# Four prologues of a gated delta rule kernel, from a counted loop to one written-out sequence

## The reference, cut to what matters

```python
    x = L0_attn_x
    xn = _layernorm(x, axis=-1)
    x = x + _L0_attn_ref(xn, ...) + _L0_ffn_ref(xn, L0_ffn_w_gate_up, L0_ffn_w_proj)
    return x
```

```python
        gu = jnp.einsum('bsd,hd->bsh', x, wq_gu)
        gate, up = jnp.split(gu, 2, axis=-1)
        h = jax.nn.silu(gate) * up
        hn = rms_norm(h)
        wq_p = ternary_quant(w_proj)
        return jnp.einsum('bsh,dh->bsd', hn, wq_p)
```

```python
            beta = jax.nn.sigmoid(b_raw.astype(jnp.float32))
            g = -A[None, None, :] * jax.nn.softplus(a.astype(jnp.float32) + dt_bias[None, None, :])
...
            g = jnp.cumsum(g.reshape(Bq, H, nc, chunk_size), axis=-1)
```

## Time and profile before

| | us |
|---|---|
| median of three runs | 5176.98 (5168.34 to 5177.32) |
| the profiled execution | 5178.37 |
| its span in the trace | 5176.3 |
| PE busy | 4793.5 (93%) |
| DVE busy | 3623.3 (70%) |
| ACT busy | 3024.5 (58%) |
| POOL busy | 1086.0 (21%) |

### The profile page before, as it was taken

One profiled execution on the slowest core, in us unless ns is written; L12 is line 12 of the kernel. 1 busy time (PEld: TensorE's weight loads), 2 busy tenths in 40 slices (PEclk: granted clock), 3 DMA queues, 4 the chain that ended last, 5 costly groups with the idle time before them and its releaser, 6 DMA issues.

```text
span 5176.3 us, 140889 instructions
## 1 busy us (share of the span) xinstructions
PE 4793.5 (93%) x52272; PEld 3332.8 (64%) x52272; DVE 3623.3 (70%) x6423; ACT 3024.5 (58%) x7909; POOL 1086.0 (21%) x1064
## 2 busy tenths in 40 slices
PE   2777799999999999999999999999999999999998
PEld 1545566666666666666666666666666666666666
DVE  6444477777777677777777767777777777777776
ACT  1222466666666656666666666666666666666665
POOL 0000122222222222222222222222222222222222
PEclk9888899999999999999999999999999999999999
DMA  1111222222222322222222222222222322222221
GB/s 50 31 30 30 82 57 64 53 54 64 57 65 52 79 63 58 64 52 55 64 57 73 68 55 63 58 65 52 57 63 68 77 52 58 61 63 58 64 52 35
DMA packets 686346, 300.56 MB, mean 58 GB/s; under 512 B 599152, under 2 KB 642288, under 8 KB 675440
## 3 DMA queue, kind: packets, MB, share of 16 engines
q1 hardware_dynamic: 546416, 283.18, 21.2%
q10 hardware_dynamic: 139264, 8.42, 1.8%
HBM read 212.76 MB, written 66.07 MB: 54 GB/s over the span
## 4 chain that ended last, share of the span: by engine, by line
issue 51%; PE 26%; POOL 12%; DVE 4%; DMA 3%; ACT 2%; SPq 1%; ACTq 1%; POOLq 0%; DVEq 0%
POOL sdec L1432 5%; PE pj L620 4%; POOL rout L1438 4%; PE dsb L757 3%; PE ms L678 2%; POOL kn L1425 2%; PE pot L570 2%; PE pj L615 2%; PE pj L549 2%; PE ms L549 2%; PE pot L715 2%; PE dsb L729 1%; PE pot L686 1%; POOL gb L1420 1%; PE pod L741 1%
## 5 line engine op out<-in xcount | busy, mean ns | idle before, releaser
L1185 DVE SCALAR_TENSOR_TENSOR cy<-xpad,cw,cy 128x1024 f32<-128x1024 f32 x768 | 1104.9, 1446 | 7.0
L620 PE MATMUL pj<-xnT,wt 128*128 128x512 f32 x2048 | 1013.4, 618 | 27.5 <-DMA xnT<-xnT_d 19.0
L1438 POOL TENSOR_TENSOR rout<-rin,expo 128x2 f32<-128x2 f32 x512 | 358.9, 701 | 2324.3 <-DVE rin L1326 2324.3
L1432 POOL TENSOR_TENSOR sdec<-st,gel 128x512 f32<-128x512 f32 x384 | 402.8, 1049 | 1148.8 <-DVE st L1315 972.0
L757 PE MATMUL dsb<-wo,yT 128*128 128x256 f32 x2048 | 573.4, 402 | 10.5 <-issue 9.4
L620 PEld LDWEIGHTS pj<-xnT,wt 128*128 128x128 f32 x2048 | 349.2, 190 | 354.4 <-issue 340.7
L915 ACT ACTIVATE xpad<-pj 128x512 f32<-128x512 f32 x512 | 304.1, 594 | 361.9 <-PE pj L620 361.9
L615 PE MATMUL pj<-wt,xnT 128*128 128x256 f32 x2048 | 509.9, 392 | 0.0
L974 ACT ACTIVATE yT<-dsb 128x256 f32<-128x256 f32 x512 | 196.6, 384 | 516.6 <-PE dsb L748 516.4
L1315 DVE TENSOR_TENSOR st<-dsb,sdec 128x512 f32<-128x512 f32 x384 | 265.1, 690 | 307.1 <-PE dsb L729 306.7
L907 ACT ACTIVATE arena<-pj 128x512 f32<-128x512 f32 x256 | 152.9, 597 | 471.1 <-issue 323.4
(11 more groups left out here) (163 smaller groups left out, 8427.8 us busy)
## 6 DMA issues: line engine op xcount, KB each, us to landing
qge<-ge_rows SPq DMA_DIRECT2D x64, 1024.0 KB, 6.9
wt<-in_L_attn_W_qkvz SPq DMA_DIRECT2D x64, 768.0 KB, 4.6
gb<-g_rows SPq DMA_DIRECT2D x128, 256.0 KB, 4.1
a_d<-at SPq DMA_DIRECT2D x64, 512.0 KB, 2.7
wo<-in_L_attn_W_out SPq DMA_DIRECT2D x64, 256.0 KB, 2.7
x_d<-xpair SPq DMA_DIRECT2D x128, 128.0 KB, 1.7
ap_<-a_d SPq DMA_DIRECT2D x512, 16.0 KB, 1.8
dd<-x_d SPq DMA_DIRECT2D x512, 16.0 KB, 1.9
```

The lines of the kernel that those rows point to most:

```text
L620: last = mm(pj[n % 2][:, :], wt[:, k, col:col + DH], batch(xnT, k, i), start=(k == 0), stop=(k == KD - 1))
L1185: stt(y, x[:, :, tap:tap + SEQ], cw[:, kind, tap:tap + 1], y, ALU.mult, ALU.add).then_inc(S["conv"], 1)
L1432: tt(sdec[:, :, :, :], st[:, c % 2, :, :, :], bc(gel[:, p, :, :].rearrange("p h (b c) -> p b h c", b=NB)[:, :, :, c], 3, DH), ALU.mult).th ...
L1438: tt(rout[:, :], rin[:, :], expo[:, 0, 0:GRP], ALU.pow).then_inc(S["routs"], 1)
```

## The change

No arithmetic changes. The loops over q are gone: every engine's instructions for the four parts stand in one sequence, with constants in place of counters, and all engines meet once, at the end. The pieces of a prologue move beside the feed-forward tiles:

- the tokens of part q+1 are loaded into the other of two buffers (`xin = (acc, base)`) while part q is in work; DVE makes their moments at tile 2 and normalizes them at tile 3, PE turns them at tiles 4 and 5, DVE splits them at tiles 6 and 7 into a second set of `xpart`;
- the decay row product of part q stands behind the gate product of tile 0, that of beta behind the gate product of tile 1, and the columns of part q come one block at a time at tiles 6, 7 and after tile 7. All three kinds go through one bank, `pod`, one after the other; the turned hidden tile keeps `pch` and `pds`;
- ACT's three exponentials of the decay move to tile 6, between Silu and the two copies;
- in the setup, the tokens of part 0 are loaded, normalized and turned first, and split between the three weight blocks; the blocks have buffers of their own and are loaded without waiting for PE;
- SP writes rows and columns first, `base_d` last, and doesn't wait for them to land before the end of part 3.

The diff, cut to its core:

On SP:

```diff
+            load_input(0)
             for n, src in enumerate((gu[0], gu[1], pr)):
-                if n:
-                    sp.wait_ge(q_pe, 4 * n)
...
+                if n == 2:
+                    sp.wait_ge(q_wb, 1)
...
-            meet(sp, 1)
-            with sp.Fori(0, NQ) as q:
...
+            save_tokens(0)
+            for q in range(NQ):
+                if q + 1 < NQ:
+                    if q:
+                        sp.wait_ge(d_bsave, 16 * q)
+                    else:
+                        sp.wait_ge(q_wb, 3)
+                    load_input(q + 1)
+                    save_tokens(q + 1)
...
                 sp.wait_ge(facc, (q + 1) * TILES)
...
+                sp.dma_start(base_d[q], xin[q % 2][:, :, :].rearrange("p t d -> p (t d)")).then_inc(d_bsave, 16)
+            sp.wait_ge(d_rows, NQ * ROWS_OUT)
+            sp.wait_ge(d_tokens, NQ * 16)
+            sp.wait_ge(d_bsave, NQ * 16)
+            meet(sp, 1)
```

On PE (ACT has the counterparts at the same places, and its three exponentials at tile 6, place 0):

```diff
+            def aside(q, t, place):
+                if (t, place) == (0, 0):
+                    decay_rows(q, 1)
+                if (t, place) == (1, 0):
+                    decay_rows(q, 0)
+                if q + 1 < NQ and t in (4, 5) and place in (0, 2):
+                    turn_tokens(q + 1, 2 * (t - 4) + place // 2)
+                if (t, place) in ((6, 2), (7, 0), (7, 2), (8, 1)):
+                    columns(q, ((6, 2), (7, 0), (7, 2), (8, 1)).index((t, place)))
+
+            for q in range(NQ):
+                for t in range(TILES + 1):
+                    if t < TILES:
+                        gate_or_up(q, t, False)
+                    aside(q, t, 0)
+                    if t:
+                        turn_hidden(q * TILES + t - 1)
+                    aside(q, t, 1)
+                    if t < TILES:
+                        gate_or_up(q, t, True)
+                    aside(q, t, 2)
+                    if t:
+                        down(q * TILES + t - 1)
```

On DVE, behind the squares of tile t and ahead of its sum:

```diff
+            def aside(q, t):
+                if t == 0:
+                    dve.wait_ge(bapr, q * 2 + 1)
...
+                    step(ts(s_a, pod[0:R64, :], dtb[:, 0:1], None, ALU.add))
+                    step(ts(s_relu, s_a, 0.0, None, ALU.max))
+                    stt(s_m, s_a, -1.0, s_a, ALU.mult, ALU.min).then_inc(mabs, 1)
+                for n in ((), (0,), (1,), (2,), (3, 4), (5,), (), ())[t]:
+                    decay_step(q, n)
+                if q + 1 < NQ:
+                    if t == 2:
+                        token_moments(q + 1)
+                    if t == 3:
+                        token_norm(q + 1)
+                    if t > 5:
+                        in_parts(q + 1, t - 6)
```

More of the change, by code:

```diff
@@ new lines, in _, with gate_or_up @@
+            pe.wait_ge(q_ev, 12)
+            def gate_or_up(q, t, up):
+                n = q * TILES + t
+                if up:
+                    if n:
+                        pe.wait_ge(fhok, 2 * n)
+                elif n:
+                    pe.wait_ge(fsil, 2 * n)
+                if not up and t % (TILES // 2) == 0:
+                    pe.wait_ge(parts, 2 * q + 1 + t // (TILES // 2))
+                for n in range(2):
+                    col = (2 * up + n) * 512
+                    for m in range(3):
+                        for k in range(KD):
+                            last = mm((ms if up else pj)[n][:, :], xpart[q % 2][m][:, k, t * P:(t + 1) * P],
+                                      wguT[:, k, col:col + 512],
+                                      start=(m == 0 and k == 0), stop=(m == 2 and k == KD - 1))
+                    last.then_inc(fgu, 1)
@@ new lines, in turn_hidden, with down @@
+            def turn_hidden(n):
+                pe.wait_ge(fhok, 2 * n + 2)
+                for i in range(FFN // P):
+                    last = tp((pch, pds)[i // 4][:, (i % 4) * P:(i % 4 + 1) * P], fh[:, i * P:(i + 1) * P], ident)
+                last.then_inc(fht, 1)
+            def down(n):
+                pe.wait_ge(fhtev, (n + 1) * 2)
+                if n:
+                    pe.wait_ge(facc, n)
+                for i in range(FFN // P):
+                    last = mm(pot[:, 0:D], fhT[:, i, :], wpT[:, i, :], start=(i == 0), stop=(i == FFN // P - 1))
+                last.then_inc(fpr, 1)
@@ L820, in _ @@
             meet(pe, 1)
-            with pe.Fori(0, NQ) as q:
-                prologue(q)
-                meet(pe, q + 2)
             head_stream(pe, front, core, weave, last_tile)
@@ L834, in _, with token_columns @@
             act.mul(nega[:, :], nega[:, :], -1.0).then_inc(o_act, 1)
+            def token_columns(q, n):
+                act.wait_ge(xnt, q * (TILES // 2) + n + 1)
+                if q and n == 0:
+                    act.wait_ge(parts, 2 * q)
+                    act.wait_ge(bapr, 2 * q)
+                    act.wait_ge(d_tokens, 16 * q)
+                fn(xnT[:, :, 2 * n * P:2 * (n + 1) * P].rearrange("p k (t c) -> p t k c", t=2),
+                   pod[:, :].rearrange("p (t k c) -> p t k c", t=2, k=KD), ACT.Copy).then_inc(xntev, 1)
+            for n in range(TILES // 2):
+                token_columns(0, n)
             for n in range(3):
@@ new lines, in aside @@
+            def aside(q, t, place):
+                if (t, place) == (1, 0):
+                    act.wait_ge(mabs, q + 1)
+                    fn(s_e, s_m, ACT.Exp).then_inc(expm, 1)
+                    act.wait_ge(bapr, 2 * q + 2)
+                    if q:
+                        act.wait_ge(colt, q * COLS)
+                    fn(beta_t, pod[0:R64, :], ACT.Sigmoid).then_inc(sigb, 1)
+                if q + 1 < NQ and t in (4, 5) and place in (0, 2):
+                    token_columns(q + 1, 2 * (t - 4) + place // 2)
+                if (t, place) == (6, 0):
+                    decay_exponents(q)
+                if (t, place) in ((6, 2), (7, 0), (7, 2), (8, 1)):
+                    column_stage(q, ((6, 2), (7, 0), (7, 2), (8, 1)).index((t, place)))
```

401 lines of the change are left out of this document (188 added, 213 removed).

## The result

The changed kernel took 5108.68 us (median of 4 runs, 5104.75 to 5113.86); the kernel before, beside it, 5177.15 (5168.34 to 5181.35). The ratio is 0.9871, 95% interval 0.9853 to 0.9888. So it is faster by 1.3%, where 2.1% was forecast: 5108.7 lies outside the range of 5060 to 5090. The profiled execution took 5113.86, the slowest of the four; its span is 5112.0.

The account below looks back on a forecast made before the run. PE bounds the tiles, a chain of other things what lies between. Last sum 101.6 us earlier, handover 6 saved, table load 1 added: 106.6 off 5178.4 gives 5071.8, median 5070.4; 5060 to 5090 holds a bit over 0.8.

Parts of the forecast that it names:

- Setup: Before part 0: first gate product at 86.9 us instead of 116.41, plus 2.2 for the clock (bounds 0 and twice that).
- the extra loads delay the tokens: Setup, rival: weight loads share the DMA engines and the tokens come last; up to 12 us, 5082; chance 0.10.
- a wait on `mabs`: Tile 1 of each part: the beta product waits for DVE's row, PE waits 2.3 us; bounds 0 and 4.9.
- The rival of one bank in the open: Turns and column blocks: half of evictions through `pod` show on PE; 19 us, 5089; chance 0.17 with short clock losses.
- Tile 3: 2.1 + 2.7 ... Nothing: DVE's pieces at tile 3 fit into the 6.44 us free per tile, so PE waits nothing for them.
- rival "Clock": Parts: new short waits lower PE's clock, 2.2 us at eight places; 18 us, 5088; chance 0.17 with one bank.
- the rival's slower side: Parts: PE stays at 1.2 of 2.4 GHz, each 9.51 tile takes twice as long; up to 5375; chance 0.02.
- handover: Last sum to first head-stream load: 6.3 us instead of 12.2, since only `base_d` is issued behind the sum; 6 saved.
- ACT's exponentials at tile 6: Tile 6: exponentials stand ahead of ACT's copies, so PE waits 0.6 us before the down product; upper bound 2.55.
- Its code is the same: Head stream: the other 4620 us, taken as unchanged except for 1.0 us of table load.
- the term of the sum: Head stream's start: a table load of 1.28 us ahead of the first decay exponential adds 1.0; bounds 0 and 1.3.
- a part that waits for its input by the size of a turnaround: Parts, rival: an overlooked wait gives back up to 25 us per part; 5095 to 5150; chance 0.03.

Follow-up runs that it names:

- filler kernel: The changed kernel with unread matmuls in PE's waits (9 before the beta product, 16 before the first token turn, 5 before a part's last turn): 5099.06 us, ratio 0.984.

## Why the prediction was wrong, point by point

**Setup: right.** Forecast 86.9 and 2.2 of clock, with 0 as the lower bound; measured 85.93 in one profile without the term, 87.02 in another with it. That the extra loads delay the tokens did not happen: DVE began the moments at 11.67, forecast 11.8. TensorE: Matmul & The Clock Gate in the Trainium skill (Part 1), by which the point of release varies between runs, agrees with these two profiles of one program. So do the two of the kernel before: its rows of part 0 took 5.89 in one and 3.65 in the other.

**The parts: most terms right, two wrong.** Tiles of 9.51, rows 1.92 each, a wait on `mabs` of 2.06 to 2.09 (forecast 2.3), part ends of 1.84 and 0.61, columns and token turns without waits for `pod`: these stand as forecast. The rival of one bank in the open fell.

The first step that failed is "Tile 3: 2.1 + 2.7 ... Nothing". I counted DVE's time per tile, where enough was left, and didn't ask when DVE reaches the piece: behind `fh` of the same tile, which is in PE's next tile. The sum of the busy times was right and the due time one tile off. It cost 10.5 us in three waits and some tenths around them, 11.0. (In the same line 5.63 - 1.76 is 3.87, not 3.75, and 99.87 to 105.33 less 1.76 is 3.70; the moments took 3.60, and nothing hangs on it.)

The second is the clock. The argument against it rested on the earlier trace rows, where a down product behind waits of 1.84 and 1.17 ran at full speed. That row was no exception. All twelve part ends in the three profiles with the old prologues have it, such as the last one of the kernel before:

```profile
541.08 3.72 PE L570 MATMUL pot<-arena 128*128 128x256 f32 x16 [1.17 <-ACT arena L872]
```

Yet in the changed kernel the same product, behind 1.84 and 0.61 or less, took 5.38, 3.72, 5.25 and 6.47 in the four parts. So what failed is the step from one kernel to another: that a wait costs nothing behind it in one sequence of work does not say so for the next, even for a shorter wait. The wait of 2.09 on `mabs` has 1.92 behind it in parts 1 and 3 and 3.49 in part 2. What tells these cases apart no run here shows. The slow products of the first profile come to 16.9 us over four parts (6.2, 1.6, 5.9, 3.2), nearly the 18 of the rival "Clock", which I held for unlikely. The filler kernel shows that without idle time in these waits nothing is lost; it does not show why some of them cost nothing. Of the rival's slower side nothing came: no part stayed at 1.2 GHz; most tiles ran in 9.51.

In sum, against the 27.1: setup -3.2, turn wait 11.0, clock 16.9, handover -1.2 (5.1 instead of 6.3), and 3.6 of small pieces, above all columns at 0.56 to 0.63 where I had 0.45, and the row products at 1.85 each from start to start, where I had 1.7.

**ACT's exponentials at tile 6: right.** The wait is 0.19, forecast 0.6. ScalarE: Activation LUTs in the Trainium skill (What ACT_TABLE_LOAD costs) would have made it 2.0; the load took 1.28 again, from 158.15 to the start of the first exponential at 159.44, with no drain to be seen, and the measurement decides.

**The head stream: wrong.** "Its code is the same" is so, and its time isn't: 15.1 us more in the profiled execution, of which only a little is the table load (1.28, at 489.56, as forecast; PE's second wait there, for ACT, is 2.10 us where it was 1.12 before, so about 1 us of it shows, the term of the sum). The sum has the clock of the head stream at no change, without a reason. Nearly all of the difference is the granted clock, as the table shows (length less losses 4604.6 before, 4606.0 after, in a spread of 4601 to 4612); why more of its waits are followed by it in the changed kernels is open.

**Range.** The 15.1 of the head stream alone would have given 5085.5, within 5060 to 5090; the 27.1 ahead of it alone 5097.5, outside. The measured median lies where I gave 0.03, to a part that waits for its input by the size of a turnaround; that is not what happened, and the turn wait is seven times smaller. That it came out faster was given 0.97.

## What to carry to other kernels

When a piece moves beside a loop, write for both engines at which step of the *other* it begins: an engine that works on the result of step t is in the other's step t+1, and room in its busy time says nothing on that. In a line of matmuls a wait of about 2 us may cost more behind it, through the clock, than it lasts: in the first profile of the changed kernel 29 us of waits had some 17 us of slow products behind them, from nothing to 3.2 us for one wait. Give it both bounds, and look at the granted clock of the stretch behind, not of the wait. That the same wait was free in the old kernel is no proof. And a stage whose code is untouched is not a constant: here it took 4621 us in the mean of three profiles and 4634 in that of ten, a difference as large as some of the terms that were worked out with care.

## What the hardware showed that was not expected

- Unread matmuls in PE's waits made the kernel faster: first load 462.91 instead of 479.87, and a median of 5099.06 us instead of 5124.77. The engine did 30 matmuls of 512 columns more in each of three parts, and 14 in the last.
- The same wait in the same program, 2.09 us, has a product of 1.92 or of 3.49 behind it, at the same place in repeated executions. So the length of a wait alone doesn't decide it; what does is open.
- The largest single losses in the parts came with the last down product of a part, 6.47 to 6.65 where 3.72 is full speed, in kernels whose waits ahead of it are the same as, or shorter than, in those where it took 3.72 (1.84, then 0.2 to 0.6). With the old prologues it took 3.72 in all twelve cases, behind the longer waits of 1.84 and 1.17.
